# Query projection of a perceiver block: sums of squares from ScalarE's accumulated output, and transposes written in the order of batch and head

## The reference

```python
# x: 8 x 64 x 512; 32 query heads of 128; eps 1e-5
def rmsnorm(x, w):                       # over the 128 of a head
    var = mean(x * x, axis=-1)
    return w * (x * rsqrt(var + eps))
h = layernorm(x)                         # 512 tokens (8 batches of 64) x 512
q = (h @ q_proj_w.T)                     # 512 tokens x 4096
q = rmsnorm(q.reshape(8, 64, 32, 128).transpose(0, 2, 1, 3), q_norm_w)
k, v = keys and values of ctx (8 x 1601 x 512), 8 heads, k normed likewise
x = x + softmax(q @ k.T / sqrt(128) + mask) @ v @ o_proj_w.T
x = x + state_space(layernorm(x))
x = x + experts(layernorm(x))
```

## Time and profile before

| | |
|---|---|
| median of three runs | 2546.01 us |
| profiled execution, its own time | 2543.32 us |
| its span, first to last instruction | 2541.5 us |
| mean granted clock of TensorE in it | 0.979 |
| PE / DVE / POOL / ACT busy, share of the span | 94% / 79% / 59% / 49% |
| last `low` of `queries` begins | at 152.27 us |
| first matmul of `cross_attention` | at 155.41 us |

### The profile page before, as it was taken

The page is one execution under the profiler, slowest core; times in us unless marked ns, Lnnn a source line. Parts: engine busy times, 40 slices in busy tenths (PEclk is TensorE's granted clock), DMA queues, the critical chain, the costliest instruction groups (busy, mean ns, idle before and its releaser), DMA issues. The chain is left out here.

```text
span 2541.5 us, 48195 instructions
## 1 busy us (share of the span) xinstructions
PE 2394.1 (94%) x18380; PEld 1736.5 (68%) x18380; DVE 1996.1 (79%) x2722; ACT 1252.1 (49%) x1830; POOL 1510.8 (59%) x927
## 2 busy tenths in 40 slices
PE   6879999999999999999999999999996878989995
PEld 3447878877887787788778878877885334544543
DVE  6868787888788778888878888888777548889984
ACT  4544554455455445544544554455443435555640
POOL 0116777777777777777777777777765003344432
PEclk9989999999999999999999999999998989999997
DMA  5521000100100010001010100100000921122100
GB/s 188 175 62 28 24 23 25 32 24 19 32 25 21 27 32 24 19 25 32 18 30 26 30 17 27 32 17 16 9 6 13 286 96 59 60 93 81 59 18 25
DMA packets 101092, 117.67 MB, mean 46 GB/s; under 512 B 8190, under 2 KB 70782, under 8 KB 100862
## 3 DMA queue, kind: packets, MB, share of 16 engines
q1 hardware_dynamic: 98846, 107.25, 13.3%
q0 software_dynamic: 2016, 7.34, 1.1%
HBM read 96.74 MB, written 17.83 MB: 45 GB/s over the span
## 5 line engine op out<-in xcount | busy, mean ns | idle before, releaser
L176 POOL TENSOR_TENSOR p_l<-S,p_h 128x1792 f16<-128x1792 f32 x126 | 422.5, 3354 | 285.9 <-ACT p_h L444 285.9
L550 DVE SCALAR_TENSOR_TENSOR S<-pS,rk,mask 128x256 f32<-128x256 f32 x832 | 359.9, 478 | 137.3 <-PE pS L244 130.6
L244 PE MATMUL pF<-w_l,ctx_h 128*128 128x256 f16 (+1 forms) x1664 | 453.5, 273 | 0.0
L244 PE MATMUL pF<-w_h,ctx_l 128*128 128x256 f16 (+1 forms) x1664 | 453.5, 273 | 0.0
L244 PE MATMUL pF<-w_h,ctx_h 128*128 128x256 f16 (+1 forms) x1664 | 453.5, 273 | 0.0
L560 DVE TENSOR_REDUCE mx<-S 128x256 f32<-128x3328 f32 x64 | 382.4, 5976 | 2.2
L244 PE MATMUL pF<-ctx_h,w_h 128*128 128x400 f16 (+1 forms) x1024 | 341.1, 333 | 4.0 <-PEq L790 4.0
L244 PE MATMUL pF<-ctx_l,w_h 128*128 128x400 f16 (+1 forms) x1024 | 341.0, 333 | 0.0
L244 PE MATMUL pF<-ctx_h,w_l 128*128 128x400 f16 (+1 forms) x1024 | 340.1, 332 | 0.0
L426 ACT ACTIVATE v_h<-pF 128x512 f16<-128x512 f32 (+1 forms) x224 | 126.7, 566 | 402.6 <-PE pF L244 402.6
L650 POOL TENSOR_TENSOR sq_l<-sq_f,sq_h 128x400 f16<-128x400 f32 (+1 forms) x256 | 242.6, 948 | 63.5 <-ACT sq_h L418 63.5
(11 more groups left out here) (256 smaller groups left out, 5498.0 us busy)
## 6 DMA issues: line engine op xcount, KB each, us to landing
ctx_p<-ctxT_dram SPq DMA_DIRECT2D x42, 458.0 KB, 3.5
s_wst<-winG_dram SPq DMA_DIRECT2D x8, 1536.0 KB, 6.5
q_wst<-wqT_dram SPq DMA_DIRECT2D x8, 1024.0 KB, 7.4
o_scratch<-o_st SPq DMA_DIRECT2D x32, 256.0 KB, 2.4
p_ost<-o_scratch SPq DMA_DIRECT2D x16, 512.0 KB, 6.6
p_wst<-woT_dram SPq DMA_DIRECT2D x16, 512.0 KB, 7.6
s_wst<-winG_dram SPq DMA_DIRECT2D x8, 1024.0 KB, 5.2
m_wost<-woutG_dram SPq DMA_DIRECT2D x8, 1024.0 KB, 5.4
```

Of the source, the lines that this page charges most:

```text
L176: eng.tensor_tensor(p_l[:, s % 2, t0:t1, :], S[:, s % 2, t0:t1, :], p_h[:, s % 2, t0:t1, :], ALU.subtract).then_inc(pl_ok, 1)
L244: mm = pe.matmul(out, x, y, start=first and j == 0, stop=final and j == 2)
L550: ins = dve.scalar_tensor_tensor(out=S[:, s % 2, t, :].rearrange("p (r q) -> p r q", r=REP), in0=bank[:, t % 2, :].rearrange("p (r q) -> p ...
```

## The change

Three edits, all in `queries`:

- The sums of squares come from ScalarE. In place of one instruction over 512 columns there are four over 128, one for each head, each with `accum_out` into its column of `ss`. DVE's reduction and the semaphore `ss_ok` are gone; ACT now waits for its own `sq_ok` ahead of the square root, and for the reciprocal of tile n - 2 ahead of the squares.
- The transposes write pR in the order batch, head, query: each output is two runs of 64 columns, 256 columns apart.
- `high` and `low` therefore read and write plain 512 columns, and `low` is one instruction in place of two.

```diff
@@ semaphores
-        ss_ok = sem("q_ss_ok")
@@ PE, turn
                 for h in range(4):
-                    mm = pe.transpose(pR[t % 2][:, h * P:(h + 1) * P], qs[:, t, h * P:(h + 1) * P], ident[:, :])
+                    mm = pe.transpose(pR[t % 2][:, :].rearrange("p (b h q) -> p h b q", b=2, h=4)[:, h, :, :],
+                                      qs[:, t, h * P:(h + 1) * P], ident[:, :])
@@ ACT, high
-                out = qh[:, j, 2 * t:2 * t + 2, :].rearrange("p b (h q) -> p h b q", h=4)
-                act.activation(out, pR[t % 2][:, :].rearrange("p (h b q) -> p h b q", h=4, b=2), ACT.Copy,
+                act.activation(qh[:, j, 2 * t:2 * t + 2, :].rearrange("p b c -> p (b c)"), pR[t % 2][:, :], ACT.Copy,
                                scale=nwp[:, 0:1]).then_inc(hi_ok, 1)
@@ ACT, body
                     wait(act, q_ok, n + 1)
-                    wait(act, ss_ok, n - 1)
-                    act.activation(sq[:, t % 2, :], pQ[t][:, :], ACT.Square, scale=1.0 / (S_H * S_W)).then_inc(sq_ok, 1)
-                    wait(act, ss_ok, n + 1)
                     wait(act, rs_ok, n - 1)
+                    for h in range(4):
+                        i = act.activation(sq[:, t % 2, h * HD:(h + 1) * HD], pQ[t][:, h * HD:(h + 1) * HD], ACT.Square,
+                                           scale=1.0 / (S_H * S_W), accum_out=ss[:, t % 2, h:h + 1])
+                    i.then_inc(sq_ok, 1)
+                    wait(act, sq_ok, n + 1)
                     act.activation(sd[:, t % 2, :], ss[:, t % 2, :], ACT.Sqrt, bias=eps2[:, 0:1],
@@ DVE, low
-                for b in range(2):
-                    mm = dve.scalar_tensor_tensor(out=out[:, b, :, :], in0=src[:, b, :, :], scalar=nwp[:, 0:1],
-                                                  in1=hi[:, b, :, :], op0=ALU.mult, op1=ALU.subtract)
-                mm.then_inc(lo_ok, 1)
+                dve.scalar_tensor_tensor(out=ql[:, j, 2 * t:2 * t + 2, :].rearrange("p b c -> p (b c)"), in0=pR[t % 2][:, :], scalar=nwp[:, 0:1],
+                                         in1=qh[:, j, 2 * t:2 * t + 2, :].rearrange("p b c -> p (b c)"),
+                                         op0=ALU.mult, op1=ALU.subtract).then_inc(lo_ok, 1)
@@ DVE, body
-                    wait(dve, sq_ok, n + 1)
-                    dve.tensor_reduce(ss[:, t % 2, :], sq[:, t % 2, :].rearrange("p (h c) -> p h c", h=4), AX.X, ALU.add).then_inc(ss_ok, 1)
                     wait(dve, sd_ok, n + 1)
```

More of the change, by code:

```diff
@@ L1055, in low @@
                 dve.wait_ge(consts, 3)
-                out = ql[:, j, 2 * t:2 * t + 2, :].rearrange("p b (h q) -> p b h q", h=4)
-                hi = qh[:, j, 2 * t:2 * t + 2, :].rearrange("p b (h q) -> p b h q", h=4)
-                src = pR[t % 2][:, :].rearrange("p (h b q) -> p b h q", h=4, b=2)
-                for b in range(2):
-                    mm = dve.scalar_tensor_tensor(out=out[:, b, :, :], in0=src[:, b, :, :], scalar=nwp[:, 0:1],
-                                                  in1=hi[:, b, :, :], op0=ALU.mult, op1=ALU.subtract)
-                mm.then_inc(lo_ok, 1)
+                dve.scalar_tensor_tensor(out=ql[:, j, 2 * t:2 * t + 2, :].rearrange("p b c -> p (b c)"), in0=pR[t % 2][:, :], scalar=nwp[:, 0:1],
+                                         in1=qh[:, j, 2 * t:2 * t + 2, :].rearrange("p b c -> p (b c)"),
+                                         op0=ALU.mult, op1=ALU.subtract).then_inc(lo_ok, 1)
             def body(pair, j):
```

## The result

The changed kernel takes 2515.22 us (median of four runs, 2513.25 to 2517.73), the kernel before in the same series 2545.16. The ratio is 0.9886, 95% interval 0.9872 to 0.99: 25 to 33 us less, against the 21 forecast. The direction is right, the time lies 1.8 us under the range's lower end of 2517.

What follows compares the result with a forecast made beforehand. VectorE's stream, with one ScalarE round trip per tile, was taken to bound `queries`; start +0.2, tiles 0-7 -7.2, tiles 8-23 -5.6, tiles 24-31 and tail -8.3 sum to -20.9 from 2546.0: 2525 us, range 2517 to 2537.

Steps and rivals of the forecast that it cites:

- the next floor: In `queries`, TensorE's own pace of matmuls and transposes: 3.02 us a tile, 12.1 a group.
- the ring through the weights: In tiles 8 to 23, chain from one group's first matmul through the weight split to the next's: 12.35 us.
- B: Stretch of `queries`, tiles 8 to 23, four groups: 49.4 us forecast against 54.95, so -5.6.
- S: ScalarE's time per tile from the first of four accumulated squares to the last's end: 1.5 us, bounds 0.8 and 2.25.
- A: Stretch of `queries`, tiles 0 to 7: 25.6 us forecast against 32.85, so -7.2.
- rival 1: Accumulation on ScalarE free or nearly, TensorE the floor: gain 26 to 27 us, time 2519; chance 0.14.
- The start: In `queries`, first squares to first reciprocal: 1.86 us forecast against 1.66, so +0.2.
- the cover of edit 1: VectorE slack of over 0.8 us a tile, hiding the cheaper `low`'s gain of 4 us except 0.3 at the end.
- C': Tile 24's reciprocal to first attention matmul; forecast 31.0 us to the last `low`, plus 1.5 to the attention.

Runs made afterwards that it cites:

- e_sums: Kernel before with only the sums of squares moved to ScalarE; old transposes, old `high` and two `low`: median 2517.5 us.
- e_order: Changed kernel with the old single square and VectorE reduction put back, new transpose order and one `low` kept: median 2542.3 us.
- e_nosum: Changed kernel with no sums: one square over 512 columns, the sums set once to a constant: median 2511.9 us.
- e_pelight: Changed kernel with two of the three query matmul products, low tokens times high weights left out: median 2507.6 us.
- c_after: The control: the changed kernel once more, with no edit: median 2518.1 us.
- e_spread: Changed kernel with context splits moved behind tiles 11, 15, 19, 23 and the last two weight splits behind 24 and 28: median 2511.7 us.
- e_fill2: Changed kernel with two more 128-column squares, without a sum, ahead of each tile's four: median 2519.3 us.
- e_fill7: Changed kernel with seven more 128-column squares, without a sum, ahead of each tile's four: median 2540.0 us.
- e_delay: Changed kernel with 46 unneeded ScalarE copies at the end of the queries, so the attention starts at 155.12 us: median 2540.8 us.
- e_spread2: Like e_spread against the changed kernel, but the two late weight splits stand behind tiles 26 and 28: median 2514.5 us.

## Why the prediction was right or wrong

**What bounds.** Right. VectorE's round with its trip to ScalarE set the pace, and taking the reduction out of it is the whole gain (e_sums, e_order). No run tells the reduction's own work from its round trip; they went together. TensorE is the next floor (12.13 us a group; e_nosum, e_pelight), and the ring through the weights is real: it is the next bound at 40.5 us for B.

**The term that was mis-sized: S.** I took 1.5 us; it is 1.14. The first kind of instruction was right, 0.16 apart for 0.17. The second was priced like another small one of 128 columns, though it has a single one; a read starts its successor 0.09 later. At 1.15 the prediction's own formulas give 7.0 us more, less what TensorE's floor takes back (A 24.2 in place of 22.8, B 48.3 in place of 48.0), about 26.2, or 2519.8 us. By its own list this was the size of rival 1, with 26 to 27 us and a chance of 0.14, but not its reason: the sum does have an instruction of its own, only a cheap one. So S accounts for 5.3 of the 9.0 us by which the saving was underrated, and by itself leaves the time inside the range. Of the rest, 1.7 lie in the stage, 1.0 of them at its start, and 2.0 behind it. The Trainium skill's rule that an accumulator output makes two instructions (VectorE: DVE Perf Modes, the section on two Vector instructions with no wait between them) is stated of VectorE; this trace shows the same on ScalarE, 128 reads for 128 squares. The estimate from the Trainium skill's ScalarE: Activation LUTs (What ACT_TABLE_LOAD costs), 1.3 us, was nearer than mine, since it took the columns out of the second instruction.

**The start, 1.3 us off.** 0.35 is S and 0.15 a first matmul that comes earlier. The rest, 0.8, is TensorE's clock. Its first query matmul starts at 19.82 before and at 19.67 after, at half pace (0.43 apart, the level of 1.2 GHz) in both. It rises to the full level at 25.77 before, with the fifteenth matmul, and already at 23.05 after:

```profile
22.63 0.63 PE L710 MATMUL q_pQ<-q_wl,q_th 128*128 128x512 f16 x1
23.05 0.50 PE L710 MATMUL q_pQ<-q_wh,q_tl 128*128 128x512 f16 x1
23.39 0.38 PE L710 MATMUL q_pQ<-q_wh,q_th 128*128 128x512 f16 x1
```

The control, with the same instructions, has its first reciprocal at 26.53. So up to 0.8 us of the first profile's gain is where the clock rose, and no merit of the change. The prediction's sum has no term for it.

**The sum as such.** At S = 1.48 the end of the stage comes within 1.6 us of it. At 2.31 the same terms give A 32.1, B 57.0, C' 38.2 and the end at 155.1; measured are 30.99, 57.86, 38.09 and 153.40. No stretch is off by more than 1.1, the start by 1.4. For the stage, what it lacked was a price, not a mechanism.

**Edits 2 and 3.** Right: no cost of the stepped transposes, nothing from the order in `high`, 0.13 us from `low`, hidden but for 0.35 us at the end. That `low` would be worth 4 us without the cover of edit 1 is not borne out: e_order's stretches give 2.6.

**The rest of the kernel, which I took as unchanged.** With the old queries the stretch behind the first attention matmul is 2388 to 2389 us in the mean (e_order, before), with new ones 2384 to 2388, although not an instruction in it differs. Part is scatter: within one kernel it spans 3 to 10 us, and it goes with the mean granted clock (over the runs of before, changed, c_after, e_sums, e_order, e_spread, e_fill2, e_fill7 and e_nosum, 2382 to 2384 us in the mean where that was 0.980 or 0.981, 2390 where it was 0.974 or 0.975).

The two profiled executions differ by 2.0 us, and these can be laid apart. Up to the first use of p_oh, a tile of the output projection, the kernel before takes 1817.5 us and the changed one 1820.1; TensorE had the lower level of its clock for 22.1 us of it before and for 28.1 after. From there to the first use of m_xc, a tile of the state space layer, it is 128.6 and 127.8. From the first to the last use of m_xc it is 388.3 and 384.7, the rest 51.6 and 51.5. So the change finds the attention 2.6 us longer and the state space layer 3.6 shorter. In the layer the clock isn't it, as the lower level stood for 23.5 us before and 23.6 after. (Where that differs the layer follows it: 386.0 us with 26.9 in e_spread, 383.0 with 21.2 in e_nosum, 383.1 with 21.3 in e_fill7.) It is one stop of VectorE, which in the kernel before comes ahead of a copy (first line) and in the changed one doesn't (second):

```profile
2268.49 0.17 DVE L1758 COPY m_parD<-m_par 128x4 f32 x1 [3.18 <-issue]
...
2239.01 0.16 DVE L1753 COPY m_parD<-m_par 128x4 f32 x1
```

"issue" is idle time in which the engine waited for nothing that the profile shows. The instruction ahead of the stop starts 26.2 us later than in the changed kernel, the copy behind it 29.5 us later. None of the other profiles has a stop there. Whether every execution of the kernel before has it isn't shown, and e_order, whose profile has none, is nearly as long in the mean (2388.4). It is not the start of the attention (e_delay), and not the pace of the queries (e_fill7 has a stage nearly as long as before). Why the means differ between kernels stays open.

**The range.** 2517 to 2537 allowed for S down to the TensorE floor but took the stretch behind and TensorE's clock at the start as fixed. Of the 30 us, 28 are the stage and 2 lie behind it, and those 2 are more than the 1.8 us by which the range was missed. The same kernel in the control series has a median of 2518.1, inside the range, so on which side of 2517 it comes out is within the scatter; that S was too large by 0.35 us is not.

## What to carry to other kernels

Moving a row sum into the ScalarE instruction that makes the squares costs a short second instruction per sum, 0.09 us here, and one instruction per sum where one did for all: the four heads take 1.14 us where a single square took 0.585. It is worth it when the reduction stood in the chain of a fuller engine together with a round trip. Price a train of small instructions by the distance between their starts, not by their rows' lengths: those overlap, and here their rows add up to nearly twice what they cost. Where the next floor is known (here TensorE's 3.02 us a tile), the gain of a step is the old round less that floor, and a change in a stage of 150 us in a kernel of 2500 is best judged at the stage's end, as the rest scatters by more than the question.

## What the runs showed of the hardware

- An activation with an accumulated output shows as two rows, ACTIVATE and ACTIVATION_READ_ACCUMULATOR; on 128 PSUM columns they start 0.16 and 0.09 us apart.
- The rows' lengths grow along an unbroken train though the starts keep their distance: the squares' mean is 0.276 us in the changed kernel, 0.295 behind two fillers, 0.347 behind seven; the reads' 0.208, 0.229 and 0.280. A row's length is no price there.
- An fp32 transpose into two runs of 64 PSUM columns, 256 apart, is as fast as into 128 in a row: 0.279 us each with it, 0.278 without (e_order, e_sums).
- VectorE can stand idle for 3 us with nothing that the profile shows it waits for, at one place in one kernel and not in another with the same instructions there: 3.18 us in the state space layer of the kernel before. In e_spread and e_spread2 it does so twice each in the attention (3.56 and 3.31, 3.35 and 3.61 us), and there the attention is no longer for it (1820.9 us in e_spread, 1821.0 in c_after, up to p_oh).
